# Expert weights in one transfer per block, begun after the last down product, in a vision tower with four layers

## The reference, cut to what matters

```python
x = hidden_states.reshape(-1, 192)
logits = x @ router_w.T
topk_w, topk_idx = jax.lax.top_k(softmax(logits), 4)
topk_w = topk_w / jnp.sum(topk_w, axis=-1, keepdims=True)
dense_w = sum(one_hot(topk_idx, 16) * topk_w[..., None], axis=1)
gate = jnp.einsum('td,eid->tei', x, w1)      # up products, 192 -> 768
up = jnp.einsum('td,eid->tei', x, v1)        # up products, 192 -> 768
act = jax.nn.silu(gate) * up
out = jnp.einsum('tei,edi,te->td', act, w2, dense_w)   # down products, 768 -> 192
```

## Time and profile before

| | |
|---|---|
| median of 3 runs | 3053.26 us (3040.43 to 3058.68) |
| the profiled execution | 3052.19 us, span 3050.1 us |
| TensorE busy | 2350.0 us, 77% of the span |
| DMA, mean | 66 GB/s |
| blocks of L1 | about 1054 to 1206 us of the span |
| blocks of L3m | about 2315 to 2520 us |
| blocks of L3f | about 2624 to 3036 us |

### The profile page before, as it was taken

How to read it: one execution, slowest core, us unless ns; L and a number is a source line. 1 busy time by engine, 2 the same in 40 slices (tenths; PEclk the granted TensorE clock), 3 DMA queues, 4 the chain that set the end, 5 groups by cost and what they waited for, 6 DMA issues and landing times. The chain is left out here.

```text
span 3050.1 us, 44650 instructions
## 1 busy us (share of the span) xinstructions
PE 2350.0 (77%) x12100; PEld 1653.3 (54%) x12100; DVE 1462.9 (48%) x3230; ACT 980.4 (32%) x2061; POOL 798.6 (26%) x781
## 2 busy tenths in 40 slices
PE   9617997975897597699779954477756993699998
PEld 9302333653675486477536722122245982699987
DVE  4269996234455311555521254899953224422222
ACT  1147784122233233233221223455522221222211
POOL 0004551001122054111100000477602441244443
PEclk9655555876676599555589976799967995799999
DMA  7000000000000386000012100000006761577775
GB/s 205 3 0 1 0 0 0 0 0 0 1 0 0 92 212 152 12 0 0 0 31 62 31 0 0 1 0 0 0 9 193 223 178 42 179 223 223 224 214 128
DMA packets 77597, 201.30 MB, mean 66 GB/s; under 512 B 17685, under 2 KB 47256, under 8 KB 69176
## 3 DMA queue, kind: packets, MB, share of 16 engines
q1 hardware_dynamic: 52472, 169.30, 17.3%
q0 software_dynamic: 25056, 31.22, 6.1%
HBM read 178.81 MB, written 22.91 MB: 66 GB/s over the span
## 5 line engine op out<-in xcount | busy, mean ns | idle before, releaser
L489 PE MATMUL bank<-g,consts 128*128 128x400 f32 (+1 forms) x640 | 388.6, 703 | 64.3 <-DVE g L628 58.6
L1502 POOL DMA_INDIRECT sums<-yblock,put x129 | 206.0, 1597 | 421.0 <-DVE yblock L1765 249.3
L622 DVE TENSOR_TENSOR_SCAN s<-bank,w 128x400 f32<-128x400 f32 (+1 forms) x320 | 313.2, 979 | 3.9 <-POOL w L597 3.8
L1550 PE MATMUL bank<-xTblock,wt 128*128 128x256 f32 (+1 forms) x1464 | 268.4, 341 | 1.7 <-ACT xTblock L1621 1.2
L1755 DVE TENSOR_TENSOR hid<-sa,bank 128x512 f32<-128x512 f32 (+1 forms) x183 | 105.9, 578 | 340.7 <-ACT sa L1642 337.8
L1575 PE MATMUL bank<-wt,hid 128*128 128x192 f32 x1548 | 265.6, 326 | 0.0
L489 PEld LDWEIGHTS bank<-g,consts 128*128 128x128 f32 (+1 forms) x640 | 117.5, 220 | 269.8 <-DVE g L628 260.1
L597 POOL TENSOR_TENSOR w<-u,spreadB 128x400 f32<-128x400 f32 x192 | 192.8, 1036 | 242.1 <-ACT spreadB L568 242.1
L1550 PEld LDWEIGHTS bank<-xTblock,wt 128*128 128x128 f32 x1464 | 237.3, 194 | 23.7 <-issue 1.6
L1575 PEld LDWEIGHTS bank<-wt,hid 128*128 128x128 f32 x1548 | 249.8, 190 | 0.2
L1642 ACT ACTIVATE sa<-bank 128x512 f32<-128x512 f32 (+1 forms) x183 | 93.3, 510 | 482.2 <-PE bank L1561 477.3
(11 more groups left out here) (364 smaller groups left out, 4062.9 us busy)
## 6 DMA issues: line engine op xcount, KB each, us to landing
wt<-L3f_packed SPq DMA_DIRECT2D x41, 1152.0 KB, 5.8
wt<-L3f_packed SPq DMA_DIRECT2D x41, 576.0 KB, 6.0
wt<-L3m_packed SPq DMA_DIRECT2D x20, 1152.0 KB, 5.6
wt<-L_packed SPq DMA_DIRECT2D x20, 579.0 KB, 4.4
wt<-L3m_packed SPq DMA_DIRECT2D x20, 577.0 KB, 5.9
wt<-L_packed SPq DMA_DIRECT2D x20, 576.0 KB
pixels<-pixels SPq DMA_DIRECT2D x16, 375.0 KB, 4.3
wu<-L_up SPq DMA_DIRECT2D x8, 576.0 KB, 4.6
```

Source lines behind the costliest of these rows:

```text
L489: nc.tensor.matmul(acc[g][0:parts, 0:CHUNK], ident[0:parts, 0:parts], g_[:, j % SLOTS, :], start=(n == 0), stop=(n == STATES - 1)).then_in ...
L622: nc.vector.tensor_tensor_scan(s[:, j % SLOTS, :], decays[j % DECAYS], w2[:, j % SLOTS, :], 0.0, ALU.mult, ALU.add).then_inc(s_done, 1)
L1502: nc.gpsimd.indirect_dma_start(t.sums, bass.IndirectOffsetOnAxis(put[:, q:q + 1], 0), y[:, b % 2, q - column_of_block[b], :], None, comput ...
L1550: nc.tensor.matmul(bank[:, n * j:n * (j + 1)], wt[:, v, cols(base, 2 * p + j)], xT[:, v, 0, 0:n], start=(j == 0), stop=False, skip_group_c ...
```

## The change

`load` issues one transfer of the whole row of `wt[:, v]` in place of two, and that one waits for block b's down products. One semaphore per buffer, `loaded[v]`, takes the place of `up_loaded[v]` and `down_loaded[v]`; TensorE waits for it ahead of `mains`, and the wait ahead of `down_` is gone. ScalarE's waits for biases and gains are on `loaded` too. The bytes moved are the same.

```diff
-                def load(at, v, up_free=None, down_free=None):
+                def load(at, v, free=None):
                     expert = sp.value_load(owner_row[0:1, at], min_val=0, max_val=E - 1)
-                    for lo, hi, free, landed in ((0, DOWN_AT, up_free, up_loaded), (DOWN_AT, WIDTH, down_free, down_loaded)):
-                        if free is not None:
-                            sp.wait_ge(*free)
-                        sp.dma_start(wt[:, v, lo:hi], packed[bass.ds(expert, 1), :, lo:hi].rearrange("a p m -> p (a m)")).then_inc(landed[v], 16)
+                    if free is not None:
+                        sp.wait_ge(down, free)
+                    sp.dma_start(wt[:, v], packed[bass.ds(expert, 1)].rearrange("a p m -> p (a m)")).then_inc(loaded[v], 16)
...
-                        load(bass.ds(b + 2, 1), v, up_free=(up_done, b * PAIRS + PAIRS), down_free=(down, b * M + 2 * M))
+                        load(bass.ds(b + 2, 1), v, free=b * M + 2 * M)
...
-                            pe.wait_ge(up_loaded[v], loads_of(first, place, i))
+                            pe.wait_ge(loaded[v], loads_of(first, place, i))
...
-                            pe.wait_ge(down_loaded[v], loads_of(first, place, i))
...
-                                act.wait_ge(down_loaded[v], loads_of(start, place, i))
+                                act.wait_ge(loaded[v], loads_of(start, place, i))
...
-                                act.wait_ge(down_loaded[1 - v], loads_of(start, place + 1, i))
+                                act.wait_ge(loaded[1 - v], loads_of(start, place + 1, i))
```

More of the change, by code:

```diff
@@ L1446, in experts @@
         added = [t.sem("added_even", lasting=True), t.sem("added_odd", lasting=True)]
-        up_loaded = [t.sem("up_loaded_even"), t.sem("up_loaded_odd")]
-        down_loaded = [t.sem("down_loaded_even"), t.sem("down_loaded_odd")]
+        loaded = [t.sem("loaded_even"), t.sem("loaded_odd")]
         turned, xT_done, up_done, silu_done, hid_done, down, y_done, y_free, shared, gate_done = (
@@ L1477, in _ @@
                         b = 2 * i + v
-                        load(bass.ds(b + 2, 1), v, up_free=(up_done, b * PAIRS + PAIRS), down_free=(down, b * M + 2 * M))
+                        load(bass.ds(b + 2, 1), v, free=b * M + 2 * M)
                 if LEAD:
-                    load(slice(B - 1, B), 0, up_free=(up_done, (B - 2) * PAIRS), down_free=(down, (B - 1) * M))
+                    load(slice(B - 1, B), 0, free=(B - 1) * M)
                 if own_gain:
                     sp.wait_ge(down, (B - 2) * M + 2 * M)
-                    sp.dma_start(wt[:, B % 2, EXTRA_AT:WIDTH], packed[0, :, EXTRA_AT:WIDTH]).then_inc(down_loaded[B % 2], 16)
+                    sp.dma_start(wt[:, B % 2, EXTRA_AT:WIDTH], packed[0, :, EXTRA_AT:WIDTH]).then_inc(loaded[B % 2], 16)
                 for b in (B - 2, B - 1):
@@ L1627, in _ @@
                 if own_gain:
-                    act.wait_ge(down_loaded[0], 16)
+                    act.wait_ge(loaded[0], 16)
                 take_xT(0, 0, subs_of[0])
```

## The result

The changed kernel takes 3103.37 us (median of 4 runs, 3099.9 to 3111.34) against 3046.85 us (4 runs) of the kernel before: a ratio of 1.0186, 95% interval 1.0141 to 1.0232. It is slower by 1.4 to 2.3%. The profiled execution took 3100.74 us with a span of 3098.9 us, 48.8 us more than the span before. (The 3053.26 us of the table ahead is the median of three of these four runs; the fourth took 3038.37 us.) The forecast was 3091 us, the range 3066 to 3120.

What follows compares the result with a forecast made beforehand. L3m and L3f were taken to run at TensorE's pace with transfers hidden, L1 nearly so. Stalls of 15.7 (L3f) + 18.0 (L3m) + 5 (L1) = 39 us on 3052.19 us gave 3091 us, range 3066 to 3120.

Steps and rivals of the forecast that it cites:

- 4.4 us to spare: L3f before the change: up weights landed at 2723.3, wanted by the big block's up products at 2727.73.
- 16, 8 and 8 places: Stalls forecast ahead of big blocks that follow a small one: 16 in L3f, 8 each in L3m and L1.
- T: Landing time of the whole joined transfer; for 1728 KB forecast at 7.4 us, low end 6.9, high end 8.3.
- L3f: 15.7 us forecast: L3f: weights landing beyond 6.42 us stall TensorE ahead of the big block, 0.98 us, 16 times.
- put at nothing: L3f and L3m: gathers are not waited for; moved weight traffic could delay them, but pairs last longer too: no cost.
- a thing that would make it wrong: The mechanism would be wrong if gaps were at other places or TensorE waited for gathers in L3f or L3m.
- L3m: 18.0 us forecast: L3m: big blocks start 2.25 us later, 8 times, as ScalarE's copy needs gains from the same transfer.
- the step over ScalarE's copy: L3m: copy starts once 1728 KB are there; 0.43 + 7.4 + 1.19 = 9.02, less 6.77: 2.25 us.
- the third rival: Stalls bring TensorE's clock down: 245 us if every stalled pair ran so, 3330 us; chance 0.03.
- L1: 5 us forecast: L1: 1155 KB landing in 5.7 us stalls the big block 1.2 us; 5 us chosen between 1 and 11.
- the low end: L1: gather's start does not hang on the stall, so the stall is spent inside the existing wait; 1 us in all.
- the high end: L1: the gather meets 1155 KB instead of 579 KB and is later by up to 1.4 us, 8 times: 11 us.

Runs made afterwards that it cites:

- the second profile of the changed kernel: The changed kernel run once more with no edit, as the measure for the other runs on that chip: 3108.49 us, ratio 1.0174 against the kernel before.

## Why the prediction was right

**Direction and mechanism.** The up weights moved from 4.4 us to spare to just too late, ahead of the big blocks that follow a small one and nowhere else: 16, 8 and 8 places, all found. The run with both transfers late shows it from the other side, since 1152 KB in time leave L3f at 19.06 us.

**T.** 7.4 us was forecast for 1728 KB. Pairs of 20.04 us, less 19.00, less the 0.10 us by which the up products behind a gap are slower (5.44 against 5.34), give a start 0.94 us later than before (the waits themselves are 12.4 / 16 = 0.78 us on average; the rest is that before, a big block began 0.17 us ahead of the end that the trace gives the products in front of it) and a T of 6.42 + 0.94 = 7.36 us, between 7.1 and 8.2 in the two issues read. The number is right, but not all the reasons. The scatters beside it were thought to be able to make it longer; without scatters it is as long. And 0.4 us of it go away when the same bytes go in two transfers, which the prediction did not name: it took T from rows of single transfers, and the price may be in these rows already. That 7.4 was met so closely within a range of 6.9 to 8.3 is in part luck. The Trainium skill's page "DMA: Bandwidth & Descriptors", in its "Rules for kernel authors", advises transfers of 1 MiB and more for bandwidth, and to make one of many small ones, which would speak for joining 576 KB to 1152 KB; the run with the load cut in two shows the joined one landing later, so at this size the trace does not agree.

**L3f: 15.7 us forecast, 16.7 measured.** On top of it came 0.9 us at the block behind the pairs, a wait for gathered rows (0.69 us at 2993.22, where the kernel before had none) that the prediction put at nothing. It is a small case of what it named as a thing that would make it wrong.

**L3m: 18.0 us forecast, 22.5 measured.** Pairs without a fall of the clock take 21.1 to 21.4 us, 2.1 to 2.4 more than 19.0; 2.25 was forecast, so the step over ScalarE's copy was right. The term that was too small is the clock: three falls of 1.7 us, 5.1 us, forecast at none. That was the third rival, with a chance of 0.03, which was too low. The argument against it took L1's gaps of 1.5 us at a granted clock of 1.00 as evidence for gaps of 2.25 us, though these were longer. Two of L1's eight were as long (2.11 and 2.30 us) and had no fall behind them; in L3m, over the two profiles of the changed kernel, 6 of 16 had one. Two cases without a fall could not have told a chance like that from none. With the falls counted as they came, the term is 23.1 us.

**L1: 5 us forecast, 6.7 measured.** The size is luck, as 5 was a choice between two ends, 1 and 11 us. The ends had two mechanisms, and both came. One pair before and one in the changed kernel, from the timelines of TensorE and GpSimd: the big block's up products, the issue of the gather and the transposes that wait for it:

```profile
1098.95 2.85 PE L1554 MATMUL bank<-xTblock,wt 128*128 128x256 f32 x12
1099.70 1.02 POOL L1497 DMA_INDIRECT xblock<-table,take  x1 [0.30 <-DVE yblock L1765]
1104.39 0.44 PE L1537 MATMUL bank<-consts,xblock 128*128 128x128 f32 x2 [1.09 <-DMA xblock<-table,take]
```

```profile
1100.84 2.85 PE L1552 MATMUL bank<-xTblock,wt 128*128 128x256 f32 x12 [0.57 <-DMA wt<-L_packed]
1100.90 1.02 POOL L1495 DMA_INDIRECT xblock<-table,take  x1 [0.30 <-DMA sums<-yblock,put]
1106.89 0.44 PE L1535 MATMUL bank<-consts,xblock 128*128 128x128 f32 x2 [1.71 <-DMA xblock<-table,take]
```

The gather does not wait for the stall: over the eight pairs its issue is 0.8 us earlier against the start of the big block's up products, which is the stall's length. But it takes 5.8 us on average from issue to the transposes where it took 5.0. So what the low end counted on was eaten by what the high end feared, and both waits stand one behind the other (5.9 us for weights, and 11.6 us for rows as before). The stall itself was 0.7 us where 1.2 was forecast. In the second profile of the changed kernel L1 took 11.7 us more than before instead of 6.7.

**The sum.** 39 us forecast (38.7 before rounding), 46.8 in the three stages by the profile: of the 8.1 us between them 5.1 are the clock, 0.9 the wait behind the pairs, 1.7 L1 and 1.0 L3f, less 0.6 in L3m. The measured ratio stands for 50 to 57 us, by which base one takes; single executions of the kernel before, in the runs of this study, spread from 3036 to 3068 us, so the last few us can't be placed.

## What to carry to other kernels

A transfer that is hidden has a slack, and a change of its place is priced by that slack: read when the buffer is wanted next by the shortest thing between, here a small block of 6.76 us, not by the average. If a late transfer must be, put first what is wanted first, and look for a second engine that takes something out of it (ScalarE's gains cost L3m more than a microsecond a pair). A gap on TensorE has a price beyond its length once the clock begins to fall behind it, and a wait for gathered rows is worth tracing to the queue in which the gather stands.

## What the runs showed of the hardware

TensorE's clock fell from 2.4 to 1.2 GHz behind some gaps as short as 1.84 us (the shortest ahead of up products that had a fall, in the run with two late transfers) in a stage in which it was otherwise always busy, while a gap of 2.52 us in L3m (in the run with 576 KB more) and one of 3.64 us in L1 (in the run with two late transfers) passed without one; in the slices behind the latter, from 1154 to 1161 us, the granted clock is 1.00. Gaps of up to 1.6 us in L3f never had one, in 16 pairs of each of two profiles of the changed kernel. A fall costs 1.7 us in L3m and L3f (7.13 against 5.44 us), and which gaps bring it differs between executions. The Trainium skill's page "TensorE: Matmul & The Clock Gate" (section "Why this matters for your kernels") warns of idle gaps between bursts of products as what brings the clock down. The traces agree that idle gaps do it, but they show it behind shorter ones than the page warns of. Filling the gaps with useless products kept the clock at 1.00.

With one transfer of 1728 KB TensorE's big block began about 0.4 us later than with the same bytes as 576 and 1152 KB issued one behind the other (pairs of 20.04 and 19.65 us), and 0.2 to 0.3 us sooner than with three of 576 KB (20.31 us). Leaving out the scatters with addition beside it did not change it (20.08 us).

In L1 a gather took 5.0 us on average from its issue to the transposes of its rows beside the weights of the kernel before, and 5.8 us beside the one transfer of 1155 KB.
